# Splitting the output product around a head's second projection, and moving its rotation between the low parts of P

## Chip, cores, metric

One core of one Trainium2 chip. The metric is the device time of one execution in microseconds (us), lower is better. The kernel before takes 588.26 us (median of three executions, 588.11 to 590.16).

## What is computed

Four blocks follow each other on an input of 2 x 512 tokens with 256 features; each is x = x + norm(block(norm(x))). The change lies in the first one, attention with 16 heads of 128, rotary position codes, a causal mask and full precision:

```
q = rope(x @ wq.T + bq);  k = rope(x @ wk.T + bk);  v = x @ wv.T + bv
attn = softmax(causal(q @ k.T / sqrt(128)))
out  = (attn @ v) @ wo.T + bo + residual
```

The three blocks behind it (a 4-bit feed-forward network, a linear attention, a second feed-forward network with looked-up weights) are untouched.

## The kernel before

**Precision.** Every value that enters a product is held as two halves, a high part (f16 of the value) and a low part (f16 of what the rounding left). `product` issues three matmuls for one: high x high, high x low, low x high. So every operand of TensorE is made twice: ScalarE writes the high part, and VectorE or GpSimd (called POOL in the profile) subtracts it from the value to give the low part.

**Units and steps.** A unit u is one head of one batch; there are 32. The loop over `STEPS` (s = -2 to 33) is a software pipeline that each engine walks through on its own, in an order written by hand in its `step(s)`; semaphores join them. The work of three units is in flight in a step. A step is counted here from the first scores matmul of its unit.

- TensorE (`step`, L1672): the four row blocks of scores of unit s (`scores`, L1606; block q first waits until low part q of P of the unit before is out of its bank, `d_pl`, and block 0 also for both low parts of q and k, `g_qkl`), first projection of unit s+2 (`project(s+2, 0)`), projection of v of unit s, output product of unit s-2 (`out_project`, L1663), second projection of unit s+2 (`project(s+2, 1)`, which waits for the first half of the rotation, `d_rope`, as both use one bank), attention times v of unit s-1 (`weigh`, L1652). In every product the moving side is 128 to 512 columns wide.
- VectorE (`step`, L1187): row maxima 0 and 1 (`top`, L1139), low part of the output o of unit s-2 (`low_o`), maxima 2 and 3, the bias and the cosine and sine products of the first projection of unit s+2 (`rotate(s+2, 0)`, L1150 and L1152), reciprocal of the sums, half of the low part of a weight (`prepare`, L1082, in some steps), low part of v (L1178), the four low parts of P of unit s (`low_p`, L1170), `rotate(s+2, 1)`, the other half of `prepare`, and, in a few steps, extra work (`low_xT0` L1076, sums and statistics, `lut_halves` L1324 to L1329).
- ScalarE (`step`, L781): high part of o, the four exponentials (L745), high part of the first rotated half of unit s+1 (`high_qk(s+1, 0)`, L767), high part of v (L772), the four high parts of P (`high_p`, L756), `high_qk(s+1, 1)`.
- POOL (`step`, L562): for unit s+1 the four additions that finish the rotation (`rotate`, L550 and L551; they wait for `d_rope`, that is for VectorE's `rotate(s+1, 1)` of the step before, and for POOL's own last subtraction), and the two subtractions of `low_qk` (L560). In steps 8 to 15 a residual addition follows (L533).
- SyncE issues the transposes of P (`turn`), one per row block once its low part is written (`d_pl`), and behind them loads of weights.

**The other batch's x.** In steps 1 and 2 TensorE also turns the other batch's x; `project(s+2, 1)` there also waits until VectorE has scaled it (`turned_x0`, L1070), since it was turned in the same bank.

Of the kernel before, what the change touches and what calls it, by code (L numbers as in the profile page):

```python
# [18 lines left out]
TPB = S // P  # L19
# [77 lines left out]
def sandwich(nc, x_in, per_head, bqT, bkT, bvT, bo, gT, bT, ropes, w1T, packed, scales, codes, lut, out):  # L97
    with ExitStack() as ctx:
# [3 lines left out]
        def sem(name):  # L102
            return ctx.enter_context(nc.semaphore(name))
# [189 lines left out]
        t_op = sem("t_op")  # L293
# [107 lines left out]
        def qk_bank(u, w):  # L401

            return o_bank if u < 2 and w else proj_bank

        def rotations(u, w):

            return 2 * u + w if u else 1

        def there(u):

            return 0 <= u < UNITS

        def head(u):

            if u < GROUP:
                return FIRST, u, u % 2
            if u < DONE:
                return OTHER, u - GROUP, u % 2
            return FIRST, u - HEADS, u % 2

        def place(b):

            return (FIRST, OTHER).index(b)
# [569 lines left out]
        def _(dve):  # L993
# [148 lines left out]
            def rotate(u, w):  # L1142
                b, h, p = head(u)
                bias = (bias_q, bias_k)[w][:, h:h + 1]
                dve.wait_ge(t_proj, 2 * u + w + 1)
                if u >= 2:
                    dve.wait_ge(g_rot, rotations(u - 2, 1))
                if u == 2:
                    dve.wait_ge(d_rot, 1)
                dve.scalar_tensor_tensor(out=turned[:, p, 2 * w, :], in0=qk_bank(u, w)[:, :], scalar=bias, in1=rope[:, 0, :],  # L1150
                                         op0=ALU.add, op1=ALU.mult)
                dve.scalar_tensor_tensor(out=turned[:, p, 2 * w + 1, :], in0=qk_bank(u, w)[:, :], scalar=bias, in1=rope[:, 1, :],  # L1152
                                         op0=ALU.add, op1=ALU.mult).then_inc(d_rope, 1)
# [13 lines left out]
            def low_p(u, q):  # L1167
                b, h, p = head(u)
                dve.wait_ge(a_ph, TPB * u + q + 1)
                dve.scalar_tensor_tensor(out=row_parts[q][:, :, 1, :],  # L1170
                                         in0=row_bank[q][:, 0:(q + 1) * P].rearrange("p (k n) -> p k n", n=P),
                                         scalar=rscaled[:, p, q:q + 1], in1=row_parts[q][:, :, 0, :],
                                         op0=ALU.mult, op1=ALU.subtract).then_inc(d_pl, 1)
# [13 lines left out]
            def step(s):  # L1187
                if there(s):
                    top(s, 0)
                    top(s, 1)  # L1190
                if there(s - 2):
                    low_o(s - 2)
                if there(s):
                    top(s, 2)
                    top(s, 3)
                if there(s + 2):
                    rotate(s + 2, 0)
                if there(s):
                    inverse(s)
                    prepare(s, (0,))  # L1200
                    low_v(s)
                if s == DONE + 4:
                    shifted(0, 0, "y")
                if s == DONE + 8:
                    shifted(0, 0, "x")
                if s in X0_TURN_AT:
                    turned_x0(OTHER, (X0_TURN_AT[s],))
                if there(s):
                    for q in range(TPB):
                        low_p(s, q)  # L1210
                if there(s + 2):
                    rotate(s + 2, 1)
                if s == -2:
                    rotated_first()
                    spread0(OTHER, range(TPB))
                if s - 1 in X0_TURN_AT:
                    low_xT0(OTHER, (X0_TURN_AT[s - 1],))
                prepare(s, (1,) if there(s) else range(2))
                if s == -1:
                    other_norms()  # L1220
                if s == UNITS - 6:
                    lut_halves()
                if s == GROUP + 1:
                    dve.wait_ge(t_op, GROUP)
                    dve.wait_ge(a_xa, place(FIRST) + 1)
                    for t in rows_of(FIRST):
                        last = dve.scalar_tensor_tensor(out=xa[:, t, :], in0=row_tile(acc_bank, t), scalar=1 / (P_SCALE * W_SCALE),
                                                        in1=xa[:, t, :], op0=ALU.mult, op1=ALU.add)
                    last.then_inc(d_part, 1)
                if s == DONE + 1:  # L1230
                    attention_sums(0)
                if s == DONE + 2:
                    for t in (0, 2):
                        tile_spread(t, nrm)
                    gathered(0, 0, "y")
                if s in (DONE + 5, DONE + 6):
                    t = 2 * (s - DONE - 5)
                    dve.wait_ge(a_y, t // 2 + 1)
                    dve.tensor_tensor(x[:, t:t + 2, :], x[:, t:t + 2, :], nrm[:, t:t + 2, :], ALU.add).then_inc(d_x0, 1)
                    dve.wait_ge(d_x0, t // 2 + 1)  # L1240
                    tile_spread(t, x)
                if s == DONE + 6:
                    gathered(0, 0, "x")
# [324 lines left out]
        def _(pe):  # L1568
# [50 lines left out]
            def project(u, w):  # L1619
                b, h, p = head(u)  # L1620
                if u == 1:
                    pe.wait_ge(d_rope, 1 + w)
                if u >= 2:
                    pe.wait_ge(d_rope, 2 * u + w)
                if w == 1 and u - 2 in X0_TURN_AT:
                    pe.wait_ge(d_xT, KC + X0_TURN_AT[u - 2] + 1)
                if u == GROUP and w == 0:
                    pe.wait_ge(d_xTl, 2 * KC)
                if is_new(u) and w == 0:
                    lows_done(h)  # L1630
                for c in range(KC):
                    ws = of_head(h, w, c)
                    xs = [a[:, c, b * S:(b + 1) * S] for a in (xTh, xTl)]
                    if u == 0 and w == 0:
                        pe.wait_ge(d_xTl, c + 1)
                    last = product(qk_bank(u, w)[:, :], ws, xs, c == 0, c == KC - 1)
                last.then_inc(t_proj, 1)
# [22 lines left out]
                    last = product(o_bank[:, k * P:S], vs, ps, k == 0, k == TPB - 1)  # L1660
                last.then_inc(t_pv, 1)

            def out_project(u):  # L1663
                b, h, p = head(u)
                pe.wait_ge(d_ol, u + 1)
                for t in range(TPB):
                    os_ = [a[:, p, t * P:(t + 1) * P] for a in (oh, ol)]
                    ws = of_head(h, 3)
                    last = product(acc_bank[t // 2][:, t % 2 * D:t % 2 * D + D], os_, ws, False, False, skip=True)
                last.then_inc(t_op, 1)  # L1670

            def step(s):  # L1672
                if there(s):
                    for q in range(TPB):
                        scores(s, q)
                if there(s + 2):
                    project(s + 2, 0)
                if there(s):
                    project_v(s)
                if s in X0_TURN_AT:  # L1680
                    pe.wait_ge(d_rope, 2 * (s + 2) + 1)
                    turn_norm0(OTHER, (X0_TURN_AT[s],))
                if s == GROUP + 2:
                    pe.wait_ge(d_part, 1)
                    open_sums()
                if s == DONE + 2:
                    pe.wait_ge(d_acc, 1)
                    open_sums()
                if s == UNITS - 1:
                    pe.wait_ge(d_rope, 2 * UNITS)  # L1690
                    turn_norm(1, 0, even_odd, (0,))
                if s == UNITS:
                    pe.wait_ge(d_xTl, TURNS.index((1, 0)) * KC + 1)
                    turn_norm(1, 0, even_odd, (1,))
                if s == UNITS + 1:
                    gate_up(0, fp4_weights(0), whole, beside_first, 0, (1,))
                if there(s - 2):
                    out_project(s - 2)
                if s == UNITS:
                    pe.wait_ge(d_pl, TPB * UNITS)  # L1700
                    pe.wait_ge(d_xTl, (TURNS.index((1, 0)) + 1) * KC)
                    gate_up(0, fp4_weights(0), whole, beside_first, 0, (0,))
                if there(s + 2):
                    project(s + 2, 1)
                if there(s - 1):
                    weigh(s - 1)

# [221 lines left out]
            for s in STEPS:  # L1929
                step(s)  # L1930
# [104 lines left out]
```

## Time and profile before

| | us |
|---|---|
| median of three executions | 588.26 |
| lowest, highest | 588.11, 590.16 |
| span of the profiled execution, first to last instruction | 586.2 |
| TensorE busy | 535.4 (91%) |
| VectorE busy | 479.2 (82%) |
| ScalarE busy | 386.5 (66%) |
| POOL busy | 382.2 (65%) |
| attention, first scores of unit 0 to first scores of unit 31 | 23.6 to 320.0 |

The profiled execution is told by its span alone; what a timed execution has around the span is the rest up to its own time, which is 2.0 us between the median and this span. In a row of a timeline the first number is the start and the second the time from start to end; behind them come engine, line, operation, tiles written and read, the number of instructions and, in brackets, how long the engine had been idle and what ended that. Instructions of one engine overlap by some hundredths of a us, so the sum of their times is a little more than the time from start to start.

### The profile page before, as it was taken

Reading aid. Unit: us, or ns where it says so; the run is one execution under the profiler, and the core shown is the slowest. Engines: PE = TensorE matmul, PEld = TensorE weight load, DVE = VectorE, ACT = ScalarE, POOL = GpSimd, SP = SyncE. Lnnn points to the kernel's source line nnn. Section 1 sums busy time; section 2 is a strip of 40 time slices with the busy share of each in tenths; the row PEclk is TensorE's granted clock in tenths of the full one; section 3 lists DMA queues with packets and bytes.
Section 4 is the critical chain, followed back from the end, with each engine's and each line's share of the span. In section 5 each row is a group of like instructions: output and inputs, shape, how many; then the busy total and the mean of one; then the engine's idle time right before and its main releaser. Section 6 shows DMA issues by size and latency. Waiting matters only on the chain.

```text
span 586.2 us, 11450 instructions
## 1 busy us (share of the span) xinstructions
PE 535.4 (91%) x4186; PEld 363.1 (62%) x4186; DVE 479.2 (82%) x949; ACT 386.5 (66%) x843; POOL 382.2 (65%) x333
## 2 busy tenths in 40 slices
PE   7569999999999999999897898899999999999895
PEld 3246666566666666666565554465688778756573
DVE  7989998999999988899997787577627796767656
ACT  4476869688877787767677856666676556556231
POOL 1767988899999798978688469732223454434432
PEclk9789999999999999999999999999999999999998
DMA  8234554547664243572433824022110000000002
GB/s 296 73 82 105 104 114 100 107 104 123 101 144 86 58 80 73 119 170 55 72 64 73 207 73 139 7 72 73 51 37 1 2 1 2 0 1 1 1 2 73
DMA packets 98457, 44.64 MB, mean 76 GB/s; under 512 B 88288, under 2 KB 90720, under 8 KB 98400
## 3 DMA queue, kind: packets, MB, share of 16 engines
q1 hardware_dynamic: 97408, 43.35, 33.2%
q8 instruction: 33, 0.54, 0.4%
q10 hardware_dynamic: 992, 0.55, 0.3%
q14 instruction: 24, 0.20, 0.1%
HBM read 21.86 MB, written 1.05 MB: 39 GB/s over the span
## 4 chain that ended last, share of the span: by engine, by line
PE 58%; DVE 17%; ACT 7%; issue 6%; POOL 5%; POOLq 0%; ACTq 0%; DVEq 0%
PE bank L1573 51%; PE bank L1753 5%; POOL qkl L583 2%; DVE parts L1170 2%; DVE nmax L1139 2%; DVE turned L1150 1%; DVE ol L1184 1%; DVE vl L1178 1%; DVE turned L1152 1%; ACT bank L745 1%; PE bank L1617 1%; POOL rr L579 1%; ACT vh L772 1%; DVE stats L1003 1%; DVE turned L1350 1%
## 5 line engine op out<-in xcount | busy, mean ns | idle before, releaser
L1573 PE MATMUL bank<-xTh,w_all_h 128*128 128x512 f16 (+2 forms) x392 | 130.3, 332 | 5.5 <-DVE xT L1070 2.4
L1573 PE MATMUL bank<-xTl,w_all_h 128*128 128x512 f16 (+2 forms) x392 | 130.0, 332 | 0.0
L1573 PE MATMUL bank<-xTh,w_all_l 128*128 128x512 f16 (+2 forms) x392 | 129.8, 331 | 0.0
L583 POOL TENSOR_TENSOR qkl<-turned,qkh 128x512 f16<-128x512 f32 (+1 forms) x44 | 54.6, 1240 | 98.3 <-ACT qkh L870 98.1
L550 POOL TENSOR_TENSOR rr<-turned 64x512 f32<-64x512 f32 x63 | 87.4, 1387 | 29.9 <-DVE turned L1152 25.8
L745 ACT ACTIVATE bank<-bank,nmax 128x128 f32<-128x128 f32 (+3 forms) x128 | 64.1, 501 | 47.8 <-DVE nmax L1139 47.4
L560 POOL TENSOR_TENSOR qkl<-rr,qkh 128x512 f16<-128x512 f32 x64 | 75.9, 1190 | 24.5 <-ACT qkh L767 22.1
L551 POOL TENSOR_TENSOR rr<-turned 64x512 f32<-64x512 f32 x63 | 82.7, 1312 | 3.7
L870 ACT ACTIVATE qkh<-turned 128x512 f16<-128x512 f32 (+1 forms) x44 | 27.6, 628 | 59.0 <-DVE turned L1350 59.0
L1170 DVE SCALAR_TENSOR_TENSOR parts<-bank,rscaled,parts 128x128 f16<-128x128 f32 (+3 forms) x128 | 64.1, 544 | 0.2 <-ACT parts L756 0.2
L1139 DVE TENSOR_REDUCE nmax<-bank 128x1 f32<-128x128 f32 (+3 forms) x128 | 57.3, 481 | 5.8 <-PE bank L1617 4.8
L1350 DVE SCALAR_TENSOR_TENSOR turned<-bank,turned 128x512 f32<-128x512 f32 (+1 forms) x44 | 29.9, 679 | 36.7 <-ACT turned L859 32.0
L1573 PEld LDWEIGHTS bank<-xTh,w_all_h 128*128 128x128 f16 (+1 forms) x392 | 38.4, 98 | 31.7 <-issue 7.1
L756 ACT ACTIVATE parts<-bank,rscaled 128x128 f16<-128x128 f32 (+3 forms) x128 | 57.1, 528 | 1.1
L1573 PE MATMUL bank<-qkh 128*128 128x128 f16 (+3 forms) x128 | 39.5, 308 | 19.9 <-issue 11.8
L1573 PEld LDWEIGHTS bank<-xTh,w_all_l 128*128 128x128 f16 (+1 forms) x392 | 38.5, 98 | 27.6 <-issue 0.3
L1573 PE MATMUL bank<-pT,vh 128*128 128x512 f16 (+3 forms) x256 | 53.9, 299 | 0.9 <-DVE vl L1178 0.8
L1573 PEld LDWEIGHTS bank<-xTl,w_all_h 128*128 128x128 f16 (+1 forms) x392 | 38.5, 98 | 17.5
L1573 PE MATMUL bank<-w_all_h,xTh 128*128 128x128 f16 x256 | 44.6, 219 | 2.4 <-DVE ol L1184 2.4
L767 ACT ACTIVATE qkh<-rr 128x512 f16<-128x512 f32 x64 | 40.3, 632 | 8.4 <-POOL rr L551 8.4
L1573 PE MATMUL bank<-w_all_l,xTh 128*128 128x128 f16 x256 | 44.5, 219 | 0.0
L1573 PE MATMUL bank<-w_all_h,xTl 128*128 128x128 f16 x256 | 44.5, 219 | 0.0
(226 smaller groups left out, 1483.3 us busy)
## 6 DMA issues: line engine op xcount, KB each, us to landing
stage<-in_per_head SPq DMA_DIRECT2D x16, 512.0 KB, 4.2
xa<-in_codes SPq DMA_DIRECT2D x32, 128.0 KB, 2.8
stage<-in_packed SPq DMA_DIRECT2D x12, 256.0 KB, 3.1
stage<-in_scales SPq DMA_DIRECT2D x12, 256.0 KB, 4.2
pT<-parts SPq DMA_TRANSPOSE x128, 2.8
stage<-in_w1T SPq DMA_DIRECT2D x2, 512.0 KB, 4.1
x<-in_x SPq DMA_DIRECT2D x4, 128.0 KB, 2.4
rope<-in_ropes ACTq DMA_DIRECT2D x1, 512.0 KB, 7.1
```

The costliest lines, as they stand in the source:

```text
L550: pool.tensor_tensor(rr[low, w, :], cos_a[part], sin_b[part], ALU.subtract)
L551: pool.tensor_tensor(rr[high, w, :], cos_b[part], sin_a[part], ALU.add).then_inc(g_rot, 1)
L560: pool.tensor_tensor(qkl[:, p, w, :], rr[:, w, :], qkh[:, p, w, :], ALU.subtract).then_inc(g_qkl, 1)
L583: pool.tensor_tensor(il[n % 2][0:rows, :], inter[0:rows, n % 2, :], ih[n % 2][0:rows, :], ALU.subtract).then_inc(g_il, 1)
L745: act.activation(row, row, ACT.Exp, bias=nmax[:, p, q:q + 1], accum_out=psum_row[:, p, q:q + 1]).then_inc(a_exp, 1)
L756: act.activation(row_parts[q][:, :, 0, :], row_bank[q][:, 0:(q + 1) * P].rearrange("p (k n) -> p k n", n=P), ACT.Copy, scale=rscaled[:, p, ...
L767: act.activation(qkh[:, p, w, :], rr[:, w, :], ACT.Copy).then_inc(a_qkh, 1)
L1139: dve.tensor_reduce(nmax[:, p, q:q + 1], row_bank[q][:, 0:(q + 1) * P], AX_X, ALU.max, negate=True).then_inc(d_max, 1)
L1170: dve.scalar_tensor_tensor(out=row_parts[q][:, :, 1, :], in0=row_bank[q][:, 0:(q + 1) * P].rearrange("p (k n) -> p k n", n=P), scalar=rsca ...
L1350: dve.scalar_tensor_tensor(out=inter[0:rows, n % 2, :], in0=U_bank[n % 2][0:rows, :], scalar=1 / (X_SCALE * W_SCALE), in1=gel[0:rows, n % ...
L1573: last = pe.matmul(dst, l, r, start=start and i == 0, stop=stop and i == 2, skip_group_check=skip)
L1753: last = pe.matmul(side_bank[1 - i][:, 0:n], spread[:, e, :], hot[pair % 2][e][:, i, 0:n], start=e == 0, stop=e == LUT // 2 - 1)
```

## The change

Two edits. On VectorE, `rotate(s + 2, 1)` stands behind the second low part of P instead of behind the fourth. On TensorE, `out_project(s - 2)` is issued in two calls: token tiles 0 and 1 stand ahead of `project(s + 2, 1)`, and tiles 2 and 3 behind it. So the product is split in steps 2 to 29 and stays whole in steps 30 to 33, where there is no unit s+2; VectorE's order differs in steps 0 to 29. The semaphore `t_op` is raised behind the last tile, as before.

```diff
@@ VectorE, step(s)
                 if there(s):
-                    for q in range(TPB):
-                        low_p(s, q)
+                    low_p(s, 0)
+                    low_p(s, 1)
                 if there(s + 2):
                     rotate(s + 2, 1)
+                if there(s):
+                    low_p(s, 2)
+                    low_p(s, 3)
@@ TensorE
-            def out_project(u):
+            def out_project(u, ts=range(TPB)):
                 b, h, p = head(u)
                 pe.wait_ge(d_ol, u + 1)
-                for t in range(TPB):
+                for t in ts:
...
-                last.then_inc(t_op, 1)
+                if TPB - 1 in ts:
+                    last.then_inc(t_op, 1)
@@ TensorE, step(s)
                 if there(s - 2):
-                    out_project(s - 2)
+                    out_project(s - 2, (0, 1) if there(s + 2) else range(TPB))
...
                 if there(s + 2):
                     project(s + 2, 1)
+                    if there(s - 2):
+                        out_project(s - 2, (2, 3))
                 if there(s - 1):
                     weigh(s - 1)
```

## Rows read from the trace of the kernel before

**Rows 1.** The page's first line.

```profile
span 586.2 us, 11450 instructions
```

**Rows 2.** The waits by engine, TensorE: total, times, longest, in us.

```profile
PE bank L1573 <- issue: 11.8, 27, 1.2
```

**Rows 3.** Busy time in two steps, 8 and 18: length, then each engine.

```profile
103.40:113.48 10.08, 9.49 (x79) 6.15 (x79) 10.08 (x22) 6.24 (x18) 8.18 (x7) 1.00 0.50 119
...
195.11:204.15 9.04, 8.88 (x77) 6.03 (x77) 8.37 (x16) 6.59 (x18) 7.71 (x6) 1.00 0.35 68
```

**Rows 4.** Timeline of TensorE, step 18 to the first scores of step 19.

```profile
199.59 0.27 PE L1573 MATMUL bank<-w_all_h,oh 128*128 128x256 f16 x1
...
200.90 0.38 PE L1573 MATMUL bank<-xTh,w_all_h 128*128 128x512 f16 x1
...
204.15 0.22 PE L1573 MATMUL bank<-qkh 128*128 128x128 f16 x1 [0.16 <-issue]
```

**Rows 5.** Timeline of ScalarE and POOL in the same stretch.

```profile
199.79 0.60 ACT L772 ACTIVATE vh<-bank 128x512 f16<-128x512 f32 x1 [0.40 <-PE bank L1573]
...
200.52 1.78 ACT L756 ACTIVATE parts<-bank,rscaled 128x128 f16<-128x128 f32 x4
...
202.17 0.64 ACT L767 ACTIVATE qkh<-rr 128x512 f16<-128x512 f32 x1
...
202.89 1.16 POOL L560 TENSOR_TENSOR qkl<-rr,qkh 128x512 f16<-128x512 f32 x1 [0.64 <-ACT qkh L767]
...
205.06 1.64 POOL L550 TENSOR_TENSOR rr<-turned 64x512 f32<-64x512 f32 x1 [1.02 <-DVE turned L1152]
```

**Rows 6.** Timeline of VectorE in the same stretch.

```profile
199.12 0.74 DVE L1152 SCALAR_TENSOR_TENSOR turned<-bank,bias_q,rope 128x512 f32<-128x512 f32 x1
...
201.76 1.91 DVE L1170 SCALAR_TENSOR_TENSOR parts<-bank,rscaled,parts 128x128 f16<-128x128 f32 x4
203.59 0.73 DVE L1150 SCALAR_TENSOR_TENSOR turned<-bank,bias_k,rope 128x512 f32<-128x512 f32 x1
...
204.91 0.67 DVE L1082 SCALAR_TENSOR_TENSOR w_all_l<-stage,w_all_h 128x512 f16<-128x512 f32 x1
205.50 0.61 DVE L1139 TENSOR_REDUCE nmax<-bank 128x1 f32<-128x128 f32 x2
```

**Rows 7.** Timeline, step 18: a POOL instruction and VectorE's prepare behind it.

```profile
199.42 1.27 POOL L551 TENSOR_TENSOR rr<-turned 64x512 f32<-64x512 f32 x1
...
199.86 1.37 DVE L1082 SCALAR_TENSOR_TENSOR w_all_l<-stage,w_all_h 128x512 f16<-128x512 f32 x1
```

**Rows 8.** Timeline of VectorE and POOL at the start of step 8.

```profile
103.64 0.68 DVE L1082 SCALAR_TENSOR_TENSOR w_all_l<-stage,w_all_h 128x512 f16<-128x512 f32 x1
103.80 1.64 POOL L550 TENSOR_TENSOR rr<-turned 64x512 f32<-64x512 f32 x1 [0.50 <-DVE turned L1152]
...
105.57 0.61 DVE L1139 TENSOR_REDUCE nmax<-bank 128x1 f32<-128x128 f32 x2
```

**Rows 9.** Timeline of VectorE and POOL at the start of step 9.

```profile
113.65 0.96 DVE L1082 SCALAR_TENSOR_TENSOR w_all_l<-stage,w_all_h 128x512 f16<-128x512 f32 x1
...
114.23 1.51 POOL L550 TENSOR_TENSOR rr<-turned 64x512 f32<-64x512 f32 x1 [0.17 <-POOL xa L533]
```

**Rows 10.** Timeline of VectorE, starts of steps 27 and 28.

```profile
280.37 1.45 DVE L1324 TENSOR_SCALAR lut_own<-lut_row 64x8 f32<-64x8 f32 x2
281.85 1.28 DVE L1327 CAST lut_h<-lut_own 128x8 f16<-128x8 f32 x1
...
291.33 0.68 DVE L1239 TENSOR_TENSOR x<-x,nrm 128x512 f32<-128x512 f32 x1
```

**Rows 11.** Timeline of TensorE and VectorE, step 2 into step 3.

```profile
54.00 0.38 PE L1573 MATMUL bank<-xTh,w_all_h 128*128 128x512 f16 x1 [1.02 <-DVE xT L1070]
...
53.77 1.91 DVE L1170 SCALAR_TENSOR_TENSOR parts<-bank,rscaled,parts 128x128 f16<-128x128 f32 x4
55.61 0.73 DVE L1150 SCALAR_TENSOR_TENSOR turned<-bank,bias_k,rope 128x512 f32<-128x512 f32 x1
...
56.92 0.68 DVE L1076 TENSOR_TENSOR xTl<-xT,xTh 128x512 f16<-128x512 f32 x1
...
58.12 0.61 DVE L1139 TENSOR_REDUCE nmax<-bank 128x1 f32<-128x128 f32 x2
```

## The prediction

> **What bounds the kernel now.** I read the page for the span [rows 1], then the waits of TensorE: apart from starts and joins it waits in one place, 27 times, 11.8 us in all, ahead of a step's first scores, with no releaser named [rows 2]. The table by stretch then shows two kinds of step [rows 3]. A regular one, like step 18, takes 9.04 us, and TensorE is busy for 8.88 of it. A late one, like step 8, takes 10.08 us, and VectorE is busy for all of it. The timelines say what ends each.
>
> Regular step: TensorE ends v's projection and starts the output product at 199.59 [rows 4]. ScalarE takes v's high part at 199.79, the four high parts of P from 200.52, the second rotated half from 202.17 to 202.81; POOL, idle until then, subtracts from 202.89 to 204.05, and 0.10 later the scores start, after a TensorE idle of 0.16 [rows 4, 5]. So the step ends by a chain that leaves TensorE at v's projection and comes back through ScalarE and POOL. Nothing that the change moves lies on it.
>
> Late step: the chain begins with the row maxima. In step 8 the first maximum starts at 105.57, 2.17 into the step, and the step takes 7.91 more [rows 3, 8]. In step 18 it started near 0.4 (TensorE's scores set that), in step 19 at 205.50, 1.35 in. From about 1.1 on (9.04 - 7.9) each us by which VectorE reaches the maxima later is a us of the step; below it nothing is lost. VectorE's work between the last projection and those maxima is what the change reorders.
>
> **Part 1, TensorE.** The output product is 12 matmuls, 199.59 to 200.90, so 1.31 us; half is 0.66 [rows 4]. In the 28 steps where it is split, the second projection starts 0.66 sooner and `weigh` at the same time as before: nothing gained or lost in regular steps. The cover is thinner: the first half of the rotation, which frees the bank, ends at 199.86 and the projection would start at 199.59 + 0.66 = 200.25 instead of 200.90 [rows 4, 6]. With the first maximum 1.35 in rather than 0.42 the rotation ends about 0.25 later, still in time; from about 1.5 in, TensorE stands here, up to 0.4 us in steps 8 and 24 to 29. That is hidden by the idle which the same lateness makes ahead of the next scores (step 8: 10.08 long, 9.49 busy, [rows 3]). The second call adds one more semaphore wait in each of 28 steps; its price is between nothing and the 0.16 of the one idle [rows 4]; I take nothing, as TensorE has that idle to spend.
>
> In step 2 it does cost. There the second projection waits for the other batch's x, until 54.00, after 1.02 us of idle [rows 11]. The output product was over before that wait and lay under it; now half of it stands behind: step 3 starts 0.66 later.
>
> **Part 2, VectorE, steps 0 to 29.** The sum of its work is unchanged; the next maxima are late only if it waits more. In step 18 the two short low parts end near 202.5, and the moved rotation needs the projection, which ends at 200.25 + 1.30 = 201.55 and is seen some 0.2 later: no stall. In regular steps low parts 3 and 4 now wait for ScalarE no more, which I price from the overlaps at 0.08 a step; it counts in six late steps (24 to 26, 28 to 30): **-0.5 us**. Where nothing moved earlier on TensorE it does stall: in step 2 the projection ends at 54.00 + 1.30 = 55.30, is seen at 55.5, while low part 2 ends near 54.5 (53.77 + 0.75) [rows 11]. One us of stall; the last low part, which was done at 55.68, ends near 58.06, the subtraction L1076 starts at 57.98 instead of 56.92, and step 3's first maximum at 59.2 instead of 58.12. That maximum stood 1.20 into its step, at the edge, so all of it counts: 1.1, and with the collision below 1.2 (the 0.66 of part 1 lies beside it): **+1.2 us**. Step 1 stalls too, but there VectorE's next `prepare` waits for POOL anyway.
>
> The low parts 3 and 4 end 1.3 us later. SyncE issues their transposes and the weight load behind them so much later; the transposes are read a whole step later. The scores of the next unit need low part 4 some 1.14 into the step; it is ready at about 0.2 in regular steps, and at 1.2 after step 4, where VectorE runs longest over: **+0.15 us** with what follows.
>
> **Part 3, what an earlier rotation triggers.** POOL's next rotation no longer waits for VectorE (1.02 us before 205.06, [rows 5]) but for its own last subtraction. It ends 0.10 ahead of the scores; a POOL instruction behind its own predecessor's semaphore starts 0.17 after that one's end [rows 9], and one more wait stands between, so POOL starts about 0.12 into the step instead of 0.33 to 0.92. That saves nothing: POOL waits for ScalarE later in the step (0.64, [rows 5]). But it meets VectorE. A subtraction of VectorE with both inputs in SBUF takes 0.67 alone and 1.37 when a POOL instruction is under way: started at 199.86 against one ending 200.69, it ended at 201.23, 0.54 after it [rows 6, 7]. Where VectorE is first, it takes 0.68 and POOL is stretched from 1.27 to 1.64 [rows 8]. Today the order is nearly always the cheap one, as POOL is released by the rotation that VectorE does just before. Now POOL at 0.12 holds until 1.39, and a VectorE subtraction asked for in between ends at 1.39 + 0.55 = 1.94:
> - step 8: asked for at 0.24, ended at 0.92 [rows 8]. It ends at 1.94: **+1.0 us**.
> - step 19: asked for at 0.76, ended at 1.43 [rows 6]. **+0.5 us**.
> - step 27: four tiny instructions in a row, of which one and then another stood out a POOL instruction each, 1.45 for two and 1.28 for one [rows 10]. POOL being first, one more instruction is stood out, less what is gained in phase: **+1.0 us**.
> - steps 9 to 16: POOL does a residual there; `prepare` already meets it (0.96, [rows 9]) and still ends in time: nothing.
> - steps 4, 6, 17, 28, 29: VectorE asks at 0.04 to 0.16, POOL at 0.12. I take VectorE to be first, as today (0.68, [rows 10]); lost, each costs 0.74 in the first three, whose maxima have slack, and 1.05 in the last two: 4.3 in all, which I keep for the range.
>
> The Trainium skill ("SBUF — State Buffer", section "Who interferes with whom") has the rule: the two engines share a port pair, whoever issues first holds it for the whole instruction, and the other fully blocks. By the page the loser's full 0.67 would follow the holder's end; the row has 0.54. By it the four collisions would cost some 0.5 us more together; the row is taken.
>
> **Sum.** +1.2 + 0.15 + 1.0 + 0.5 + 1.0 - 0.5 = +3.4 us on the profiled execution's span, 586.2 to 589.6; with the 2.0 between that span and the median of the runs, 591.7 us.
>
> **Rivals.**
> - *Every close race is lost too*: +4.3, 596.0 us. For it: my start of POOL is good to 0.1 only.
> - *The collisions don't come, or the stall is absorbed*: only part of the start-up cost is left, about +1, 589.3 us. For it: POOL may need more time between its two waits than I give; POOL at 0.25 or later loses to `prepare` in step 8 and in all close races.
> - *The new wait decides*: the second projection stands for its bank, and that is not hidden: nine late steps by 0.3 on top of the sum, 594.4 us. Against it: TensorE idles in just those steps.
> - *Faster*: POOL's head start carries through to its second subtraction, and TensorE's wait ahead of the scores goes. 24 steps by 0.16 is 3.9, 584.4 us. It decides from the point at which that subtraction starts before 202.89, in step 18's terms. Against it: it starts when ScalarE's copy ends, and POOL had idled 0.64 before it [rows 5].
>
> **How the numbers follow.** Forecast 0.50 (589 to 593 by itself), all races lost 0.14, no collisions 0.22, the new wait 0.06, faster 0.08. A measurement can tell about 0.5% from no change, 2.9 us: the bounds are 585.3 and 591.2. Of the forecast, 0.35 lies over 591.2. Slower: 0.35 + 0.14 + 0.06 = 0.55. Same: 0.15 + 0.22 = 0.37. Faster 0.08. The range leaves out the faster case and the tails: 588.3 to 596.0.
>
> **What would show it.** Regular steps still 9.04 long, with 0.16 of idle. In step 2 the second projection still starts behind a wait on L1070, half of the output product behind it, and L1150 waits there for TensorE for about 1 us. POOL's L550 starts 0.1 to 0.15 into the step, with no wait on L1152. The L1082 of steps 8 and 19 takes 1.2 to 1.7 us rather than 0.67. Prediction wrong: if L1082 at a step's start is still 0.67 in both, if a regular step is shorter than 9.0, or if the first maximum in late steps comes no later than before.

## Result and the profile after

The changed kernel takes 591.03 us (median of 22 executions, 589.81 to 593.34), the kernel before, measured beside it, 589.37 us (22 executions, 585.34 to 592.44). The ratio is 1.0036, 95% interval 1.0019 to 1.0053: slower by 0.36% or 2.1 us (the medians differ by 1.7), where the forecast was 591.7 us and +3.4. The step is real but smaller than the 0.5% that I had set as the bound of "same". The median is nearer to the forecast than the difference is, since the kernel before, measured again beside it, took 1.1 us more than the 588.26 from which I had started.

The page's first line and the waits of TensorE in the changed kernel, with total, times and longest in us:

```profile
span 589.5 us, 11450 instructions
```

```profile
PE bank L1576 <- issue: 10.9, 28, 1.2
...
PE bank L1576 <- DVE xT L1070: 2.6, 2, 1.7
...
PE bank L1576 <- DVE turned L1152: 1.8, 7, 0.7
```

Against [rows 1] the span is 3.3 longer. The wait ahead of the scores is no longer than in [rows 2]; the third line is what changed: a projection stands for its bank seven times, 1.8 us in all, where it was twice and 0.9. The table of three steps (8, 17 and 18: length, then PE, PEld, DVE, ACT and POOL busy, the granted clock, DMA) is the one to compare with [rows 3]:

```profile
106.90:116.74 9.84, 9.44 (x78) 6.04 (x79) 9.84 (x22) 6.26 (x18) 8.35 (x7) 1.00 0.51 116
189.24:198.91 9.67, 9.06 (x76) 5.90 (x77) 9.22 (x17) 7.58 (x19) 7.73 (x6) 1.00 0.36 70
198.92:207.96 9.04, 8.88 (x76) 6.01 (x77) 8.25 (x17) 6.30 (x18) 7.70 (x6) 1.00 0.35 68
```

Step 18 is what it was, 9.04 with TensorE busy for 8.88. Step 8 is 9.90 from scores to scores (the window is cut 0.05 short), where it was 10.08 and I had forecast 11.1. Step 17, a regular 9.04 before, is 9.67. So the forecast of its mechanism holds in some places and has the wrong sign in others; the steps must be compared one by one. Steps are measured from first scores to first scores:

```
steps              before   after   difference   forecast
4 to 5              18.76   18.72     -0.04       +0.15
6                    9.04    9.68     +0.64        0 (a close race)
8                   10.08    9.90     -0.18       +1.0
17                   9.04    9.67     +0.63        0 (a close race)
19                   9.26    9.68     +0.42       +0.5
24 and 25           19.29   19.37     +0.08       -0.16
27                  11.17   10.69     -0.48       +1.0
26, 28, 29, 30      38.27   37.86     -0.41       -0.3
the others         129.00  128.88     -0.12
all from 4 to 30   253.91  254.45     +0.54
```

What is left of the 3.3 lies ahead of step 4, which started at 66.04 and now starts at 68.89; behind step 31 the two are alike within 0.1. The experiments split those 2.85.

**Step 17, a lost race.** POOL and VectorE in the changed kernel around 189.24, the first scores of step 17:

```profile
187.98 1.16 POOL L560 TENSOR_TENSOR qkl<-rr,qkh 128x512 f16<-128x512 f32 x1
189.27 1.26 POOL L550 TENSOR_TENSOR rr<-turned 64x512 f32<-64x512 f32 x1
...
188.16 1.26 DVE L1170 SCALAR_TENSOR_TENSOR parts<-bank,rscaled,parts 128x384 f16<-128x384 f32 x2
189.34 1.75 DVE L1082 SCALAR_TENSOR_TENSOR w_all_l<-stage,w_all_h 128x512 f16<-128x512 f32 x1
191.01 0.61 DVE L1139 TENSOR_REDUCE nmax<-bank 128x1 f32<-128x128 f32 x2
```

POOL begins 0.13 after the end of its own subtraction, no longer held by L1152 [rows 5]. VectorE asks 0.07 later and needs 1.75 instead of 0.67 [rows 6]: POOL ends at 190.53, VectorE 0.56 after that. The first maximum stands 1.77 into the step instead of 0.76, and the step is 0.63 longer.

**Step 8, a won one.** The same place in step 8:

```profile
106.88 1.84 POOL L550 TENSOR_TENSOR rr<-turned 64x512 f32<-64x512 f32 x1
...
106.91 0.68 DVE L1082 SCALAR_TENSOR_TENSOR w_all_l<-stage,w_all_h 128x512 f16<-128x512 f32 x1
```

VectorE asks 0.03 after POOL's recorded start and is still served first; POOL is stretched to 1.84. Compare [rows 8].

**Step 24, given back.** ScalarE in the changed kernel, high parts of P of step 24:

```profile
261.27 1.62 ACT L756 ACTIVATE parts<-bank,rscaled 128x128 f16<-128x128 f32 x3
263.22 0.69 ACT L756 ACTIVATE parts<-bank,rscaled 128x512 f16<-128x512 f32 x1 [0.33 <-DMA pT<-parts]
```

The fourth high part waits for a transpose of the step before, which was not expected anywhere. Step 24 grows by 0.81, but VectorE works on meanwhile and step 25 shrinks by 0.73. The transpose stands on the queue behind eight loads of the 4-bit weights, which land up to 4.0 into step 24, and lands later or earlier from run to run. The fourth transpose of step 23 landed 7.76 into step 24 here; in three of the runs below with the same VectorE order there (experiments 4, 5 and 9) at 7.46 to 7.54, and step 24 took 10.02 to 10.10; in three others (3, 8 and 10) at 6.45 to 6.78, and step 24 took 9.46 or 9.47. The pair of steps is 19.19 in all six.

### The profile page after: what moved, and what is told of

The parts are those of the page before. It is cut to its first block, busy times and chain, and to the rows that moved or that the text cites. A ratio compares the mean times of both kernels' runs of the same rounds, so it can differ in the third digit from the quotient of the medians.

```text
span 589.5 us, 11450 instructions
## 1 busy us (share of the span) xinstructions
PE 537.9 (91%) x4186; PEld 361.9 (61%) x4186; DVE 480.8 (82%) x949; ACT 386.4 (66%) x843; POOL 382.1 (65%) x333
## 3 DMA queue, kind: packets, MB, share of 16 engines
HBM read 21.86 MB, written 1.05 MB: 39 GB/s over the span
## 4 chain that ended last, share of the span: by engine, by line
PE 54%; DVE 20%; ACT 7%; issue 6%; POOL 5%; DMA 1%; SPq 0%; POOLq 0%; ACTq 0%; DVEq 0%
PE bank L1576 48%; PE bank L1759 5%; DVE parts L1170 3%; POOL qkl L583 2%; DVE turned L1150 2%; DVE turned L1152 2%; DVE nmax L1139 2%; DVE w_all_l L1082 2%; DVE ol L1184 1%; DVE vl L1178 1%; ACT bank L745 1%; DMA pT<-parts 1%; POOL rr L579 1%; DVE stats L1003 1%; PE bank L1620 1%
## 5 line engine op out<-in xcount | busy, mean ns | idle before, releaser
L550 POOL TENSOR_TENSOR rr<-turned 64x512 f32<-64x512 f32 x63 | 85.0, 1349 | 22.6 <-DVE turned L1152 16.3
```

The lines of the kernel that those rows point to most:

```text
L550: pool.tensor_tensor(rr[low, w, :], cos_a[part], sin_b[part], ALU.subtract)
```

## The experiments

All times of stretches are from the trace of one profiled execution, ratios from the repeated ones. Short names: steps 4 to 31 means from the first scores of step 4 to those of step 31, 253.91 us before.

**Experiment 1: TensorE's edit alone.**

```diff
 VectorE, step(s), back to the old order
-                    low_p(s, 0)
-                    low_p(s, 1)
+                    for q in range(TPB):
+                        low_p(s, q)
                 if there(s + 2):
                     rotate(s + 2, 1)
-                if there(s):
-                    low_p(s, 2)
-                    low_p(s, 3)
```

> Only TensorE's edit: the output product is split around the second projection, VectorE keeps the old order. My theory (the cost sits in VectorE's stalls at the start and in its collisions with POOL): regular steps 9.04 us, the first scores of step 3 come 0.66 later than in the kernel before but the row maxima of step 3 do not, so step 4 starts as before; span 586.2 +- 0.5, ratio 1.000. Rival (the thinner cover or the 28 added waits of TensorE cost): late steps grow by some 0.3 us each, span 588.5 to 589.5, ratio 1.004 or more.

Measured: ratio 0.9995 (0.9967 to 1.0022); steps 4 to 31 254.00, 0.09 more than before. The late steps have not grown: step 8 is 10.08, step 27 11.18. The rival falls; the thinner cover and the 28 added waits cost nothing. The span of this profiled execution, 589.1, is no answer, since TensorE's clock was at half from 44.4 to 47.9 in it, a third stretch that the kernel before did not have in its own; experiment 6 takes up step 2.

**Experiment 2: VectorE's edit alone.** The output product is whole and ahead of the second projection again.

> Only VectorE's edit: the rotation stands behind the second low part of P, TensorE keeps the whole output product ahead of the second projection. My theory: VectorE now waits about 0.6 us for TensorE in each regular step (projection seen at 7.3 into the step, second low part done at 6.66); that is hidden in steps without prepare and costs 0.2 to 1.4 us in steps 9, 11, 12, 14, 15; span 590.5 to 594, slower than the changed kernel by 1 to 4 us. Rival (VectorE's order alone makes the whole cost, the split is worth nothing): span 589.5, as the changed kernel.

Measured: ratio 1.0133 (1.0112 to 1.0154), span 595.3, steps 4 to 31 259.85, 5.9 more than before and 5.4 more than with both edits. VectorE in a regular step (10) of this run:

```profile
133.72 0.73 DVE L1170 SCALAR_TENSOR_TENSOR parts<-bank,rscaled,parts 128x128 f16<-128x128 f32 x2
135.08 0.75 DVE L1150 SCALAR_TENSOR_TENSOR turned<-bank,bias_k,rope 128x512 f32<-128x512 f32 x1 [0.62 <-PE bank L1576]
```

The wait is 0.62 where 0.6 was forecast. It is hidden in steps without `prepare` and costs elsewhere. Against the changed kernel it is 0.3 in steps 11 and 14, 0.6 in step 4, 0.9 in steps 24 and 25 together, and about 1.1 in steps 8, 28 and 29; the first maxima of steps 4, 8, 28 and 29 now come late behind lost races. The rival (the split is worth nothing) falls: the two edits belong together. The total lay outside my 590.5 to 594, as I had not counted the late steps.

**Experiment 3: POOL held behind the last low part of P.**

```diff
 POOL, rotate(u)
                 pool.wait_ge(d_rope, 2 * u + 2)
+                if u >= 2:
+                    pool.wait_ge(d_pl, TPB * (u - 1))
```

> The changed kernel, with one more wait on POOL: its rotation of unit u also waits until the last low part of P of unit u-2 is written, so POOL starts behind VectorE's subtraction as in the kernel before. My theory (collisions on the way to SBUF make steps 6, 17 and 19 late): L1082 at their start takes 0.67 again, steps 6 and 17 are back at 9.04 and step 19 at 9.2, late steps keep their 0.1 us of gain; span 587.5 to 588.2, i.e. 1.3 to 2.0 below the changed kernel. Rival (steps 6, 17 and 19 are late for another reason, such as the transposes or the weight loads): no change or slower, since POOL gets less time, span 589.5 or more.

Measured: step 6 9.04, step 17 9.04, step 19 9.27, steps 4 to 31 253.18, that is 1.27 below the changed kernel and 0.73 below the kernel before. POOL and VectorE at the start of step 17 in this run (first scores at 190.15):

```profile
190.47 1.59 POOL L552 TENSOR_TENSOR rr<-turned 64x512 f32<-64x512 f32 x1 [0.42 <-DVE parts L1172]
...
190.25 0.68 DVE L1084 SCALAR_TENSOR_TENSOR w_all_l<-stage,w_all_h 128x512 f16<-128x512 f32 x1
```

VectorE is first again and takes 0.68; nothing else in these steps was changed. That settles the cause of steps 6, 17 and 19. The time did not follow: ratio 1.0034 (1.0014 to 1.0054), span 589.9. Step 1 took 13.77 instead of 11.80, with a half-clock stretch from 45.8 to 49.2 in it. The four other profiled executions with such a third stretch (experiments 1, 2, 6 and 9) have step 1 at 13.69 to 14.01 without the added wait, so most of this goes with the clock. The wait holds POOL in steps 1 to 3 too, where it had a use for its head start (see the start-up cost below); what that costs in the time is not shown. And step 27 went to 11.29, from 10.69: there POOL's head start pays (see step 27 below).

**Experiment 4: both edits from step 4 on.**

```diff
 VectorE and TensorE, step(s)
+                early = there(s) and there(s + 2) and s >= 4
...
+                    out_project(s - 2, (0, 1) if there(s + 2) and s >= 4 else range(TPB))
```

> The changed kernel with the old orders of both engines in steps 0 to 3. My theory: steps 1 to 3 lose the two 1 us stalls of VectorE and the 0.66 of TensorE; step 4 starts at 66.0 to 66.4 instead of 68.9, the later steps are as in the changed kernel; span 586.7 to 587.3. Rival (the start-up difference is the clock of the first 40 us and not the order): step 4 still starts near 68.5 and the span is 589.

Measured: ratio 1.0010 (0.9988 to 1.0033), span 586.5; step 4 at 65.97, steps 4 to 31 254.24. Step 4 starts 2.92 sooner than in the changed kernel, as my theory had it. But the rival about the clock was only half wrong: about 1.2 of it goes with the placement of the half-clock stretches, as experiment 5 shows.

**Experiment 5: both edits in step 7 and from step 23 on.** The same switch with `s == 7 or s >= 23`.

> Both edits, but only in step 7 and from step 23 on; the old orders elsewhere. My theory (the change pays only where a late step begins with VectorE work that does not lose the way to SBUF to POOL): step 8 is 0.18 shorter, steps 24 to 30 together 0.8 to 1.1 shorter, all others as before; span 585.0 to 585.3, ratio 0.998. Rival (the gain of the late steps is given back behind the attention, or comes from the head start of earlier steps): span 586.2, ratio 1.000.

Measured: steps 24 to 30 67.68 against 68.73, 1.05 shorter as expected. But step 8 was 11.00, not 9.90, and steps 4 to 31 253.71; span 587.2 and ratio 1.0018 (0.9990 to 1.0047), both above what I had expected. POOL and VectorE at the start of step 8 in this run (first scores at 104.61):

```profile
104.65 1.26 POOL L550 TENSOR_TENSOR rr<-turned 64x512 f32<-64x512 f32 x1
...
104.86 1.60 DVE L1082 SCALAR_TENSOR_TENSOR w_all_l<-stage,w_all_h 128x512 f16<-128x512 f32 x1
106.38 1.41 DVE L1230 SCALAR_TENSOR_TENSOR xa<-bank,xa 128x256 f32<-128x256 f32 x4
107.71 0.61 DVE L1139 TENSOR_REDUCE nmax<-bank 128x1 f32<-128x128 f32 x2
```

This is the collision of my forecast to the letter: VectorE asks 0.24 into the step, POOL holds since 0.03, the first maximum comes at 3.10. In the changed kernel it did not happen, as VectorE asked at 0.06. There POOL had its head start in step 7 too (0.03 into it, against 0.32 here, where step 6 keeps the old order), so the `prepare` in the middle of step 7 took 0.66 instead of 0.83, and VectorE came out 0.18 sooner. 0.18 us decides about 1.1.

This run has a second use. Its steps 0 to 3 are those of the kernel before, instruction by instruction, and yet its step 4 starts at 67.24 and not 66.04. The stretches (length, PE, PEld, DVE, ACT, POOL busy, then the granted clock) of the kernel before:

```profile
21.20:21.80 0.60, 0.00 (x0) 0.00 (x0) 0.60 (x2) 0.60 (x3) 0.60 (x1) 0.50 0.00 0
28.00:28.60 0.60, 0.60 (x4) 0.25 (x3) 0.03 (x1) 0.53 (x1) 0.58 (x1) 1.00 0.00 0
```

and of this run; the changed kernel has the same granted clock as this run in both:

```profile
21.20:21.80 0.60, 0.00 (x0) 0.00 (x0) 0.60 (x2) 0.60 (x3) 0.60 (x1) 1.00 0.00 0
28.00:28.60 0.60, 0.60 (x3) 0.27 (x2) 0.12 (x1) 0.44 (x1) 0.60 (x1) 0.50 0.00 0
```

In all of them the clock falls to its lower level (1.2 of 2.4 GHz) twice ahead of 40 us, each time after TensorE had stood idle, but 0.8 later in this run and in the changed kernel, and so under other matmuls. With the same instructions, that placement is all that I find between the two for the 1.20 by which step 4 moves. Three more profiled executions have the old orders in steps 0 to 3 and two such stretches, and they fit it. From first scores to first scores, steps 0 to 3 took 42.42 us with the first stretch beginning 3.1 us ahead of them (experiment 4), 42.52 with 2.4 (the kernel before), 42.64 with 2.2 (experiment 8), 43.63 with 1.6 (this run) and 43.77 with 1.2 (experiment 10). No run moved the clock alone, so this is agreement and not proof. Against this run the changed kernel's start-up costs 68.89 - 67.24 = 1.65 us.

**Experiment 6: the output product split in step 2 only, VectorE's order old.**

> The kernel before with one change: the output product of step 2 is split around the second projection; VectorE's order is the old one everywhere. Theory A (the 0.66 of TensorE lies beside VectorE's work): the scores of step 3 start 0.66 later than in the kernel before, measured from the scores of step 2, but those of step 4 at most 0.1 later; ratio 1.000. Theory B (the half product is a cost of its own): step 4 is 0.6 later too, ratio 1.001.

Measured: from the first scores of step 2 to those of step 4 20.23 us, 19.84 before: step 2 grew by 0.44, step 3 shrank by 0.07. The half-clock stretches of this execution are over as step 2 starts. The half product is in it in full: from the second projection that waited for L1070 to the scores of step 3 it is 3.57 us (56.88 to 60.45), where it was 2.92 (54.00 [rows 11] to 56.92). The other 0.2 came back because the `prepare` in the middle of step 2 took 1.37 instead of 1.58. So B: where VectorE doesn't stall, the half product is a cost of its own, 0.65 us. Ratio 1.0032 (1.0009 to 1.0055), 1.9 us, more than either figure would give; the rest I can't place.

**Experiment 7: the moved rotation in steps 1 and 2 only, TensorE's order old.**

> The kernel before with one change: VectorE's rotation stands behind the second low part of P in steps 1 and 2 alone, where TensorE's second projection waits for the other batch's x. Theory A (VectorE's two stalls there, with the collisions that follow, are the start-up cost): VectorE waits about 1 us for TensorE in each of the two steps, step 4 starts 2.0 to 2.8 us later than before (66.0) if the granted clock dips as often, span 588.2 to 589, ratio 1.004. Theory B (the stalls are absorbed, the cost came with TensorE's part or the clock): below 1 us, ratio 1.001 or less.

VectorE's waits in this run:

```profile
46.01 0.75 DVE L1150 SCALAR_TENSOR_TENSOR turned<-bank,bias_k,rope 128x512 f32<-128x512 f32 x1 [0.99 <-PE bank L1576]
...
56.61 0.75 DVE L1150 SCALAR_TENSOR_TENSOR turned<-bank,bias_k,rope 128x512 f32<-128x512 f32 x1 [0.99 <-PE bank L1576]
```

Two waits of 0.99, and step 4 starts at 69.41, 2.17 after that of experiment 5, whose clock fell at the same times. Span 589.6, ratio 1.0072 (1.0043 to 1.0101), more than the 1.004 that I had expected. Theory A holds in part. The stall of step 1 costs nothing: step 1 is 12.20 and step 2 10.60, against 12.23 and 10.73 in experiment 5. All of the cost is in step 3, 11.38 against 9.11, behind the stall of step 2 and a collision. TensorE's half product lies beside it when both are there: from the first scores of step 2 to those of step 4 this run takes 21.98 us and the changed kernel 21.96.

**Experiment 8: both edits from step 4 on, POOL held only where it wins otherwise.** Experiment 4, and the wait of experiment 3 with `if u in (6, 7, 18, 20)`.

> Both edits from step 4 on, and POOL held back behind the last low part of P only where it otherwise wins the way to SBUF (starts of steps 5, 6, 17 and 19). My theory: steps 5, 6, 17, 19 as in the kernel before (9.6, 9.04, 9.04, 9.27), step 8 at 9.90, steps 24 to 30 as in the changed kernel; span 584.9 to 585.3, ratio 0.998. Rival (other steps lose what these gain): span 586 or more.

Measured: steps 4 to 31 252.40, 1.51 below the kernel before; steps 5, 6, 8, 17 and 19 at 9.73, 9.05, 9.91, 9.05 and 9.05. Each of these steps is at its time in the kernel before or below it, as the theory wants it. But the span is 587.1, where I had expected 584.9 to 585.3, and the ratio 1.0006 (0.9986 to 1.0027).

**Experiment 9: both edits from step 23 on.** The switch of experiment 5 without step 7.

> Both edits from step 23 on, the old orders up to step 22. My theory: step 8 is back at 10.08 (its 11.00 in the run with step 7 changed was a lost race of VectorE's subtraction), steps 24 to 30 together take 67.7 instead of 68.7 as their first maxima come 0.1 to 0.5 sooner; step 4 to step 31 takes 252.9 against 253.9; ratio 0.998 to 0.999. Rival (the gain of steps 24 to 30 needs the steps ahead in the new order): 253.9.

Measured: ratio 0.9974 (0.9952 to 0.9995), 587.74 us against 589.21; step 8 10.07, steps 24 to 30 67.67, steps 4 to 31 252.79. This is the one kernel of the study that is faster than the kernel before beyond its interval; the changed kernel stood at 1.0036 against the kernel before measured beside it. With ten kernels measured, one interval that ends at 0.9995 says little by itself; the firmer sign is the trace, 1.12 us between steps 4 and 31.

**Experiment 10: the kernel of experiment 8 again.**

> The same kernel as the run before last (both edits from step 4 on, POOL held at the starts of steps 5, 6, 17 and 19), again, for its time. My theory: step 4 to step 31 takes 252.4 again, 1.5 below the kernel before; ratio 0.9975 on average, where the granted clock dips as often as in the kernel before. Rival (the gain in the trace does not reach the time, or is paid back by more dips): ratio 1.000 or more.

Measured: steps 4 to 31 252.46; ratio 0.9985 (0.9956 to 1.0013), 588.49 against 589.21. The trace repeats within 0.1, the time is not told from no change. The mean granted clock of each timed execution tells where the gain went. Of the executions at 0.984, the 12 of this kernel (experiments 8 and 10) took 588.6 us on average and the 7 of the kernel before measured beside them 590.3: 1.7 less, much as in the trace. But 17 of this kernel's 24 executions have a mean clock of 0.985 or less, and 13 of 58 of the kernel before. So the rival's second half stands: the gain is paid back by more time at half clock. The profile shows where some of that lies. The same 3.2 us behind the attention, first in the kernel before, then in this run (the granted clock is the third number from the end):

```profile
329.90:333.10 3.20, 3.09 (x20) 1.72 (x19) 3.20 (x3) 2.88 (x4) 2.33 (x2) 1.00 0.86 199
```

```profile
329.90:333.10 3.20, 3.20 (x15) 1.98 (x13) 3.20 (x3) 2.33 (x3) 2.37 (x2) 0.50 1.04 226
```

Both profiles of this kernel have a half-clock stretch there, and those of the others have none; from step 31 to the end it takes 267.7 us, and the kernel before 266.3. Why the clock falls there in this kernel alone was not tried.

## Why the prediction was right and where it was not

**The structure held.** Regular steps are 9.04 with both edits, and TensorE still idles for 0.15 or 0.16 at their ends, since the chain through v's projection, ScalarE and POOL has nothing of the change on it; TensorE's edit alone is worth nothing from step 4 on (experiment 1), and the split is what keeps VectorE's moved rotation from waiting (experiment 2, a wait of 0.62). The rival "the new wait decides" is refuted: the wait is there, seven times, and lies under idle time, as step 17's 9.67 with 9.06 busy shows. The gain of 0.08 a step is there in steps 26 and 28 to 30 (0.08 to 0.13); the +0.15 for the fourth low part was -0.04.

**The collisions are real and cost what was said.** Lost, one costs VectorE about 1.1 us, of which the slack of the step takes its part: +0.64, +0.63 and +0.42 in steps 6, 17 and 19 (forecast for a lost one: 0.74, 0.74, 0.5). Experiment 3 takes away nothing but POOL's head start, and all three are gone.

**Who wins was forecast badly, and this is the step that failed.** I put POOL's start at 0.12 into the step from [rows 9]; it was 0.03, since the gap behind its own subtraction was 0.13 and not 0.17 with one wait more. By that start all five close races would have been POOL's. Three were VectorE's all the same (steps 4, 28 and 29, asked for at 0.03), because VectorE is served first even 0.03 after POOL's recorded start; at 0.07 it is not. The trace of the kernel before had both cases already, in the middle of steps 4 and 13:

```profile
70.72 1.27 POOL L551 TENSOR_TENSOR rr<-turned 64x512 f32<-64x512 f32 x1
70.79 1.74 DVE L1082 SCALAR_TENSOR_TENSOR w_all_l<-stage,w_all_h 128x512 f16<-128x512 f32 x1
```

```profile
154.60 1.82 POOL L551 TENSOR_TENSOR rr<-turned 64x512 f32<-64x512 f32 x1
154.63 0.67 DVE L1082 SCALAR_TENSOR_TENSOR w_all_l<-stage,w_all_h 128x512 f16<-128x512 f32 x1
```

And in step 8 I took VectorE's request from the kernel before, 0.24, though POOL's head start also shortens the `prepare` in the middle of step 7 and so brings that request forward to 0.06 (experiment 5). The term of +1.0 was -0.18.

**Step 27 had the wrong sign.** VectorE and its four tiny instructions in the changed kernel (first scores at 284.21):

```profile
284.60 1.12 DVE L1327 TENSOR_SCALAR lut_own<-lut_row 64x8 f32<-64x8 f32 x2
285.75 1.12 DVE L1330 CAST lut_h<-lut_own 128x8 f16<-128x8 f32 x1
286.91 0.17 DVE L1332 TENSOR_TENSOR lut_rest<-lut_own,lut_h 128x8 f32<-128x8 f32 x1
```

In [rows 10] two of them waited out a POOL instruction each, 1.45 and 1.28 in all. Here it is two again, not three, and each wait is shorter, because POOL had started earlier: the first tiny instruction waits for POOL's first and the second slips in right behind it (1.12 for the two), and the third waits 1.12. My sum counted one more POOL instruction waited out, and it should have asked at what point of POOL's rhythm VectorE arrives. Held later by 0.3 (experiment 3), VectorE waits out two again and the first maximum is at 3.39, later even than before (3.26).

**The start-up cost was undersized.** The stall in step 2 is 0.99 as forecast, L1150 waiting for TensorE. The step-1 stall is absorbed, as I took it: it puts step 2's first maximum at 1.79 instead of 0.59, but in experiment 7, with the same stall and that maximum at 1.80, step 2 takes 10.60, no longer than before. That step 2 is 11.25 in the changed kernel, 0.52 longer than before, is TensorE's half product (0.65 against experiment 7). It makes no difference two steps on, since VectorE is the later one in step 3. There comes a collision that I had priced at 0.1, and this is the term that was too small. VectorE in the changed kernel, step 2 into step 3 (first scores at 58.17), against [rows 11]:

```profile
54.37 0.73 DVE L1170 SCALAR_TENSOR_TENSOR parts<-bank,rscaled,parts 128x128 f16<-128x128 f32 x2
56.09 0.75 DVE L1150 SCALAR_TENSOR_TENSOR turned<-bank,bias_k,rope 128x512 f32<-128x512 f32 x1 [0.99 <-PE bank L1576]
...
58.60 0.79 DVE L1076 TENSOR_TENSOR xTl<-xT,xTh 128x512 f16<-128x512 f32 x1
59.31 1.74 DVE L1082 SCALAR_TENSOR_TENSOR w_all_l<-stage,w_all_h 128x512 f16<-128x512 f32 x1
60.98 0.61 DVE L1139 TENSOR_REDUCE nmax<-bank 128x1 f32<-128x128 f32 x2
```

L1082 takes 1.74 instead of 0.68: between the two subtractions POOL got its second instruction in. So the collision costs 1.06 and not 0.1; with the 1.1 of the stall that is the 2.1 us by which the changed kernel is longer from the first scores of step 2 to those of step 4 (21.96 against 19.84). Step 3 is 10.71 instead of 9.11. Against experiment 5, step 1 is 0.43 shorter (11.80 against 12.23), as POOL's head start lets the `prepare` ahead of the other batch's x end sooner, so that the whole is 1.65 where 1.2 was forecast. The sum came that near only because this gain, which I had not counted, stood against the collision.

**SyncE.** I had the transposes issued 1.3 us later. They aren't: in steps 20 to 26, which I compared, the fourth is issued 10.1 to 11.2 into the step and never later than in the kernel before (10.1 to 12.1), some 0.8 or more behind the last low part (9.2 to 9.9). The queue issues one transpose some 1.3 us after the other, and was late already.

**The sum was better than its terms.** +1.65 at the start, +0.54 in steps 4 to 30 and -0.1 behind make +2.1, which is what the repeated executions show. That the profiled span came out at 589.5 against my 589.6 is luck: it has 1.2 us of clock placement in it, which no term of mine was about, and two terms of +1.0 that were -0.18 and -0.48.

**The signs.** Of those that I had named, the wait of about 1 us in step 2, the regular steps and the missing wait on L1152 from step 4 on are there (step 5 shows L1152 ahead of the same gap of 0.13). L1082 took 1.39 at the start of step 19, but 0.68 at that of step 8, and L550 starts at 0.03. One sign of a wrong prediction is nearly met: the first maximum comes earlier than before in 8 of the 10 late steps (5, 8, 19, 24 to 30), and later only in 5 and 19. So the time came out near the forecast while late steps behaved mostly the other way.

## What to carry to other kernels

When work is moved earlier, list whose start was tied to it, and ask what that engine, now starting sooner, meets: here a faster release of POOL cost VectorE 1.1 us wherever POOL got to SBUF first. Price such a meeting by the trace, but give the order of arrival a chance of its own where the two are within 0.2 us, and work it out from the new timeline, not from the old one. And an order that gains 0.1 us in steps which are late anyway can be confined to them: experiment 9 did that in one condition and is the only version whose interval lies below 1.

## What the runs showed that I had not expected

- VectorE's subtraction goes first although POOL's instruction has a recorded start 0.03 earlier (step 8, POOL then 1.84), and goes second when it is 0.07 earlier (step 17). The twelve traces of this study hold without exception to a line between the two: the 45 subtractions L1082 and L1076 recorded 0 to 0.04 behind POOL's start took 0.66 to 0.68, the 34 recorded 0.06 to 0.30 behind it 1.41 to 1.75. The loser's time is the rest of the holder's plus 0.54 to 0.56, against 0.67 alone.
- In the first 50 us TensorE's clock falls to its lower level for two or three short stretches. With those 0.8 us later against the work, step 4 started 1.2 us later, and the executions of the kernel before spread from 585.23 to 593.72 with mean clocks from 0.993 to 0.978. A change of 0.2% in this kernel can be read in the trace from step 4 on, and hardly in the time, unless executions of equal mean clock are compared (experiment 10).
- The moved order left the issue of the DMA transposes where it was, but the fourth of step 23, behind the weight loads, landed anywhere from 5.9 to 7.8 us into step 24 in the twelve traces; the latest stretched that step by 0.8, which was given back in the next.
